# Attention and top-2 expert kernel on one core: order of the shared and routed iterations, scatter pacing and offset loads

## The reference

```
q, k, v = x Wq' + bq, x Wk' + bk, x Wv' + bv     # 8 query heads, 2 key/value heads of 16
attn    = softmax over the last 32 positions, with a sink term in the denominator
x       = layernorm(x + attn(q, k, v) Wo' + bo)
shared  = (silu(x sw1) * (x sw2)) sw3            # 128 -> 256 -> 128
probs   = softmax(x rw + rb); keep the best 2 of 8 experts, weights scaled to sum 1
routed  = sum over the 2 experts of weight * (silu(x ew1) * (x ew2)) ew3
x       = layernorm(x + shared + routed)
```

## Time and profile before

| what | us |
|---|---|
| three timed runs | 234.68, 229.27, 235.91 |
| their median | 234.68 |
| the profiled execution, its own time | 228.97 |
| its span, first to last instruction | 227.2 |
| PE busy | 171.9 (76% of the span) |
| POOL busy | 98.6 (43%) |
| mean granted TensorE clock | 0.932 of full speed |

### The profile page before, as it was taken

The page is one execution under the profiler, slowest core; times in us unless marked ns, Lnnn a source line. Parts: engine busy times, 40 slices in busy tenths (PEclk is TensorE's granted clock), DMA queues, the critical chain, the costliest instruction groups (busy, mean ns, idle before and its releaser), DMA issues.

```text
span 227.2 us, 3459 instructions
## 1 busy us (share of the span) xinstructions
PE 171.9 (76%) x974; PEld 119.0 (52%) x974; DVE 111.8 (49%) x360; ACT 107.8 (47%) x229; POOL 98.6 (43%) x110
## 2 busy tenths in 40 slices
PE   7499598698686657699678999999999899960000
PEld 2096577677574534456345656566666465650000
DVE  7875498589659929658123112121221221894070
ACT  2578968867945521312023555565556455650000
POOL 8440001006722766635700156465565544688330
PEclk9969999999999996999799999999999999996555
DMA  5995000000110111426530022333322036003310
GB/s 114 356 437 228 3 1 1 3 0 12 54 32 0 40 54 35 117 62 139 134 82 0 3 69 61 110 94 84 77 61 70 12 103 210 15 21 115 109 57 23
DMA packets 19458, 18.17 MB, mean 80 GB/s; under 512 B 3027, under 2 KB 17754, under 8 KB 19312
## 3 DMA queue, kind: packets, MB, share of 16 engines
q1 hardware_dynamic: 16432, 13.28, 20.2%
q0 software_dynamic: 2496, 4.24, 5.9%
q10 hardware_dynamic: 512, 0.45, 0.6%
HBM read 11.47 MB, written 7.39 MB: 83 GB/s over the span
## 4 chain that ended last, share of the span: by engine, by line
PE 47%; DVE 15%; issue 12%; POOL 7%; ACT 6%; DMA 5%; another core or an unknown queue 4%; ACTq 1%; POOLq 0%; DVEq 0%; SPq 0%
PE gu L574 18%; PE att L472 5%; POOL z_rows L1202 5%; PE q_bank L612 4%; PE att L586 3%; PE att L612 3%; PE att L566 3%; DMA bias<-biases 3%; PE q_bank L597 3%; PE att L552 2%; PE att L488 2%; ACT qT L706 2%; DVE mx L884 2%; DVE x L933 2%
## 5 line engine op out<-in xcount | busy, mean ns | idle before, releaser
L1202 POOL DMA_INDIRECT z_rows<-y,xin x46 | 45.6, 992 | 48.2 <-ACT y L790 36.6
L574 PE MATMUL gu<-w,xt 128*128 x92 | 45.7, 617 | 4.1 <-DVE h L1037 1.2
L1040 DVE TENSOR_TENSOR h<-sil,gu 128x512 f32<-128x512 f32 (+1 forms) x24 | 15.9, 663 | 61.8 <-ACT sil L776 57.1
L1194 POOL DMA_INDIRECT x_list<-x,pos x32 | 31.4, 981 | 16.5 <-issue 8.5
L776 ACT ACTIVATE sil<-gu 128x512 f32<-128x512 f32 (+1 forms) x24 | 13.9, 579 | 29.1 <-PE gu L574 26.8
L574 PEld LDWEIGHTS gu<-w,xt 128*128 128x128 f32 x92 | 15.5, 189 | 19.9 <-issue 19.9
L472 PE MATMUL att<-kM,qT 96*128 96x128 f32 x128 | 17.6, 297 | 8.2 <-ACT kM L719 3.6
L472 PEld LDWEIGHTS att<-kM,qT 96*128 96x128 f32 x128 | 16.4, 209 | 9.7 <-issue 9.7
L488 PE MATMUL att<-vbd,probT 128*128 128x128 f32 x128 | 17.1, 282 | 4.2 <-ACT probT L751 2.9
L1166 POOL TENSOR_TENSOR vareps<-mv,eps 128x4 f32<-128x4 f32 x4 | 0.8, 200 | 44.6 <-DVE mv L926 44.6
L488 PEld LDWEIGHTS att<-vbd,probT 128*128 128x128 f32 x128 | 15.3, 191 | 6.0 <-issue 3.6
(11 more groups left out here) (116 smaller groups left out, 289.0 us busy)
## 6 DMA issues: line engine op xcount, KB each, us to landing
w<-weights SPq DMA_DIRECT2D x1, 3456.0 KB, 16.6
xin<-x_list SPq DMA_DIRECT2D x46, 65.0 KB
z<-z_rows SPq DMA_DIRECT2D x3, 512.0 KB
x_list<-blank SPq DMA_DIRECT2D x18, 65.0 KB, 2.4
out<-result SPq DMA_DIRECT2D x3, 256.0 KB, 2.3
z_rows<-y,xin POOLq DMA_INDIRECT x46
xT<-x_cols SPq DMA_DIRECT2D x2, 256.0 KB, 5.7
xr<-x_rows SPq DMA_DIRECT2D x2, 256.0 KB, 7.0
```

What stands on the lines that cost most here:

```text
L574: mm = pe.matmul(gu_half[q], xt[:, pair % 2, q * P:(q + 1) * P], w[:, bass.ds(at[first_tile(pair) + q], CT)], start=True, stop=True)
L1040: dve.tensor_tensor(blocks(h[:, i % RING, 0:n * HIDDEN], HIDDEN), blocks(sil[:, i % 2, 0:n * HIDDEN], HIDDEN), blocks(gu[:, 0:n * CT], CT) ...
L1194: pool.indirect_dma_start(x_list[PART_OF[n]][:, :], bass.IndirectOffsetOnAxis(ap=pos[:, n, k, j:j + 1], axis=0), x2[:, n * ROWT + j, k * R ...
L1202: pool.indirect_dma_start(z_rows[g][:, :], bass.IndirectOffsetOnAxis(ap=xin[:, r, q, R_ID:R_ID + 1].bitcast(U32), axis=0), y[:, r, q, :], ...
```

## The change

1. The two shared iterations of chunk 3 go from iterations 6 and 7 to 30 and 31, behind the last pair. Pairs are now iterations 6 to 29; their number, and the 32 iterations, are the same. The first of the two moved iterations uses the banks post and att[3], the second gu; their sums go to x_bank (att[0]) instead of q_bank. PE does down_routed of the last pair ahead of the last up_shared, ACT scales the last two pairs in iteration 31, and add_shared(3) stands behind DVE's loop.
2. In scatter(n) POOL waits, ahead of the fifth of the 8 DMAs, until the first four of this chunk have landed.
3. PE loads the weight offsets for each pair (2 values, 24 loads), one iteration ahead, instead of 31 and 15 values at once.
4. rank(2) on PE goes ahead of the first up_shared. On DVE turn(3) goes ahead of read_ends(0), and make_table(0) goes from ahead of iteration 0 into iteration 1, behind hidden(1). The rest of chunk 3 (scale1, transpose, route, logits, rank, gates, places, table 1) goes one iteration later.
5. The combines of pieces 0 to 2 go to iterations 26, 27 and 28, scale2 to 28, 29 and 30; on POOL rstd2_of stands behind pairs 17, 18 and 19.

```diff
-SHARED_ITERS = 2 * CHUNKS
-R_AT = [SHARED_ITERS, SHARED_ITERS + PAIRS[0]]
-ITERS = R_AT[1] + PAIRS[1]
+FIRST_SHARED = 2 * (CHUNKS - 1)
+R_AT = [FIRST_SHARED, FIRST_SHARED + PAIRS[0]]
+R_END = R_AT[1] + PAIRS[1]
+ITERS = R_END + 2
...
-        gu_shared = [gu_half, [att[2][:, :], att[3][:, :]]]
+        turns = [gu_half, [att[2][:, :], att[3][:, :]]]
+        ends_banks = [[post[:, :], att[3][:, :]], gu_half]
...
+        SUMS_AT = R_AT[1] + 4
...
-            def fetch_weights(g):
-                pe.wait_ge(table_done, g + 1)
+            def fetch_weights(pair):
+                g, t = part_of(pair), first_tile(pair)
+                if t == 0:
+                    pe.wait_ge(table_done, g + 1)
                 _, values = nc.values_load_multi_w_load_instructions(
-                    table[g][0:1, T_W:T_W + TILES[g]], engines=PE_ONLY, min_val=0, max_val=SHARED * WRAW,
+                    table[g][0:1, T_W + t:T_W + t + width(pair)], engines=PE_ONLY, min_val=0, max_val=SHARED * WRAW,
...
             def up_shared(i, n, t):
                 pe.wait_ge(x2T_sb, n + 1)
                 after(pe, h_done, i - 1)
+                if i == R_END:
+                    pe.wait_ge(pos_done, CHUNKS)
+                    pe.wait_ge(step_done, 13)
...
+            rank(CHUNKS - 2)
             up_shared(0, 0, 0)
-            rank(CHUNKS - 2)
...
             for i in range(ITERS + 2):
-                if i == R_AT[0] - 1:
-                    at = fetch_weights(0)
-                if i == R_AT[1] - 1:
-                    next_at = fetch_weights(1)
-                if i + 1 < ITERS and pair_of(i + 1) is not None:
+                if pair_of(i + 1) is not None:
+                    at[i + 1] = fetch_weights(pair_of(i + 1))
                     turn_rows(pair_of(i + 1))
+                if i == ITERS - 1:
+                    down_routed(pair_of(i - 2), at[i - 2])
...
-                if i == 2:
+                if i == 3:
                     transpose_x2(last)
-                if i == 3:
+                if i == 4:
                     route(last)
-                if i == 4:
+                if i == 5:
                     rank(last)
...
-            read_ends(0)
             turn(last)
-            make_table(0)
+            read_ends(0)
             for i in range(ITERS):
                 hidden(i)
                 if i == 0:
                     norm1(last)
                 if i == 1:
+                    make_table(0)
+                if i == 2:
                     scale1(last)
-                if i == 3:
+                if i == 4:
                     logits(last)
-                if i == 4:
+                if i == 5:
                     gates(last)
                     places(last)
                     read_ends(1)
                     make_table(1)
...
-                if R_AT[1] + 5 <= i < R_AT[1] + 8:
-                    combine(i - R_AT[1] - 5)
-                if i == R_AT[1] + 7:
-                    scale2(0)
-            scale2(1)
-            scale2(2)
+                if SUMS_AT <= i < SUMS_AT + 3:
+                    combine(i - SUMS_AT)
+                if SUMS_AT + 2 <= i < SUMS_AT + 5:
+                    scale2(i - SUMS_AT - 2)
+            add_shared(last)
...
                 for j in range(first, last):
                     for k in range(2):
+                        if (j, k) == (2, 0):
+                            pool.wait_ge(scattered[PART_OF[n]], 16 * (2 * ROWT * PARTS[PART_OF[n]].index(n) + 4))
...
             for pair in range(PAIRS[0] + PAIRS[1]):
                 scatter_results(pair)
-                if PAIRS[0] + 3 <= pair < PAIRS[0] + 6:
-                    rstd2_of(pair - PAIRS[0] - 3)
+                piece = pair + FIRST_SHARED + 3 - SUMS_AT
+                if 0 <= piece < 3:
+                    rstd2_of(piece)
```

More of the change, by code:

```diff
@@ L114, in shared_of @@
 def shared_of(i):
-    return (i // 2, i % 2) if 0 <= i < SHARED_ITERS else None
+    if 0 <= i < FIRST_SHARED:
+        return i // 2, i % 2
+    return (CHUNKS - 1, i - R_END) if R_END <= i < ITERS else None
 def pair_of(i):
-    return i - SHARED_ITERS if SHARED_ITERS <= i < ITERS else None
+    return i - FIRST_SHARED if FIRST_SHARED <= i < R_END else None
 def part_of(pair):
@@ L565, in up_shared @@
                 for part in range(2):
-                    mm = pe.matmul(gu_shared[i % 2][part], w[:, at + part * HIDDEN:at + part * HIDDEN + P], x2T[:, tokens(n)],
+                    mm = pe.matmul(gu_shared(i)[part], w[:, at + part * HIDDEN:at + part * HIDDEN + P], x2T[:, tokens(n)],
                                    start=True, stop=True)
@@ L574, in up_routed @@
                     mm = pe.matmul(gu_half[q], xt[:, pair % 2, q * P:(q + 1) * P],
-                                   w[:, bass.ds(at[first_tile(pair) + q], CT)], start=True, stop=True)
+                                   w[:, bass.ds(at[q], CT)], start=True, stop=True)
                 mm.then_inc(up_mm, 1)
@@ L593, in down_shared @@
                         pe.wait_ge(q_sb, queries_done(CHUNKS - 1))
-                    after(pe, base_done, n)
+                    if n == CHUNKS - 1:
+                        pe.wait_ge(xt_sb, PAIRS[0] + PAIRS[1])
+                    else:
+                        after(pe, base_done, n)
                 at = SHARED * WRAW + DOWN + t * D
                 for j in range(ROWT):
-                    mm = pe.matmul(q_bank[:, j * D:(j + 1) * D], h[:, i % RING, j * P:(j + 1) * P], w[:, at:at + D],
+                    mm = pe.matmul(shared_sums(n)[:, j * D:(j + 1) * D], h[:, i % RING, j * P:(j + 1) * P], w[:, at:at + D],
                                    start=t == 0 and j == 0, stop=t == 1 and j == ROWT - 1)
@@ L690, in _ @@
                     down_shared(i - 2, *shared_of(i - 2))
-                elif pair_of(i - 2) is not None:
-                    down_routed(pair_of(i - 2), at if i - 2 < R_AT[1] else next_at)
+                elif pair_of(i - 2) is not None and i < ITERS - 1:
+                    down_routed(pair_of(i - 2), at[i - 2])
         @block.scalar
@@ L763, in rows_turned @@
                 act.wait_ge(xt_mm, pair + 1)
-                after(act, up_mm, SHARED_ITERS + pair - 1 if pair >= 2 else 0)
+                after(act, up_mm, FIRST_SHARED + pair - 1 if pair >= 2 else 0)
                 n = width(pair) * P
@@ L772, in silu @@
                 if shared_of(i) is not None:
-                    act.activation(sil[:, i % 2, :], gu_shared[i % 2][0], ACT.Silu).then_inc(silu_done, 1)
+                    act.activation(sil[:, i % 2, :], gu_shared(i)[0], ACT.Silu).then_inc(silu_done, 1)
                 else:
@@ L780, in hidden_turned @@
                 act.wait_ge(ht_mm, pair + 1)
-                after(act, down_mm, SHARED_ITERS + pair - RING + 1 if pair >= RING else 0)
+                after(act, down_mm, FIRST_SHARED + pair - RING + 1 if pair >= RING else 0)
                 n = width(pair) * HIDDEN
@@ L835, in _ @@
             last = CHUNKS - 1
-            for i in range(ITERS + 3):
+            for i in range(ITERS):
                 if pair_of(i + 1) is not None:
@@ L840, in _ @@
                     rows_out(i - 3, pair_of(i - 3))
-                if i < ITERS:
-                    silu(i)
-                if i == 2:
+                if i == ITERS - 1:
+                    rows_out(i - 2, pair_of(i - 2))
+                silu(i)
+                if i == 3:
                     x2T_out(last)
@@ L1131, in _ @@
             places(last - 1)
+            turn(last)
             read_ends(0)
-            turn(last)
-            make_table(0)
             for i in range(ITERS):
```

20 lines of the change are left out of this document (13 added, 7 removed).

## The result

The changed kernel takes 219.17 us in the median of four runs (217.12 to 223.27), the kernel before 231.98 in four (228.25 to 235.91). The ratio is 0.951, with a 95% interval of 0.939 to 0.962: 5% faster, some 12 us. The forecast was 219, 0.92 on faster.

What follows compares the result with a forecast made beforehand. PE alone bounds pair 0 to 20 (70.6 us), with holes before it and POOL's scatters in the tail. Pair 0 starting 13.0 us earlier takes 228.97 to 216.0; 2.9 for the median gives 219, range 212 to 228.

Steps and rivals of the forecast that it cites:

- The sum: Whole kernel: 13.0 us off 228.97, from pair 0 starting at 104.0 instead of 116.96, gives 216.0.
- The 2.9 added for the median: Whole kernel: half of the 5.7 us by which the median lay above the profiled execution, making 219.
- The rows' chain: Ahead of pair 0: table 0, POOL's scatters, first load of rows at 96.6 instead of 100.11, rows there at 99.2.
- the pause: POOL's scatters: waiting after four frees PE's held signals, removing gaps of 3.5 and 3.3 us; 1 lost to 5.1 gained.
- Deferred iterations: Chunk 3's two shared iterations, moved behind the last pair: 5.5 us gained before pair 0, hidden in the tail.
- Offsets by pairs: PE's 24 small loads during the pairs: 0.34 us for two values, all hidden; bounds 0 to 12.7 us.
- the hole at 108.5: PE's idle spell at the load of 31 offsets, with the slow clock after it: 4.5 us gained.
- The check's terms: Ahead of pair 0: 5.5 us shared iterations, 4.5 hole with slow clock, 3.0 earlier rows, as a check on 13.0.
- The rival of held signals that stay: Before chunk 3's ranks: pause doesn't remove the gaps, only 5 to 7 us gained, 226 us; chance 0.25.
- Between pairs 0 and 1: Start of the pairs: 0.5 us added because DVE has places(3) and table 1 between two iterations' products.

Runs made afterwards that it cites:

- e6: The changed kernel, same code, run and profiled again: 217.93 us in the profiled execution, median 217.78, ratio 0.950.
- e12: The changed kernel with up_shared(5), rank(3), down_shared(3) ahead of turn_rows(0), silu(5) ahead of rows_turned(0), make_table(0) ahead of iteration 0, pause kept: 0.966, median 216.94 us.
- e7: The changed kernel with chunk 3's shared iterations put back to iterations 6 and 7: median 224.59 us, profiled execution 222.21.
- e3: The kernel before with only the offsets loaded by pairs: ratio 0.988 (0.979 to 0.996).
- e4: The changed kernel with the 31 and 15 offsets loaded at once again: ratio 0.965 (0.952 to 0.977).
- e5: The kernel before, unchanged, run again for its trace: 233.38 us.
- e2: The changed kernel without the pause in the scatters: ratio 0.963 (0.952 to 0.975).
- e10: The changed kernel without the pause, run again in a later call: ratio 0.959 (0.952 to 0.966).
- e11: The changed kernel without the pause, with up_shared(5), rank(3), down_shared(3) ahead of turn_rows(0), silu(5) ahead of rows_turned(0), make_table(0) ahead of iteration 0: 0.946, median 211.73 us.
- e9: The kernel before with the pause alone, run again in a later call: median 227.22 us beside 229.59 for the kernel before.
- e1: The kernel before with only the pause after four scatters added: ratio 1.010 (1.003 to 1.017), some 2 us slower.

## Why the prediction was right, point by point

**The sum.** Forecast 216.0 for an execution like the profiled one; e6, which is one, took 217.93. Pair 0 begins at 105.21, forecast 104.0. From pair 0 to 20 there are 71.6 instead of 70.6, from there to the last scatter 23.3 instead of 23.7: 11.75 - 1.0 + 0.4 are the 11.0 us between 228.97 and 217.93, within 0.2. So the sum was 1.9 us too low. The 2.9 added for the median was too much: the median of 219.17 is 1.2 above e6. That 219 was met within 0.2 is luck, two errors that cancel.

**The rows' chain.** Table 0 was ready at 87.95 (forecast 88.5), last scatter of part 0 issued at 94.53 (93.8), first load of rows at 97.55 (96.6), rows there at 100.2 (99.2). That PE would then wait for rows, 3.0 us forecast, was 2.56. Right, with a shift of 0.7 to 1.0 from POOL. A part of it is the pause of chunk 2: I had booked nothing for it, and POOL waited 0.93 us (90.63 in e6), 3.28 in e12.

**Deferred iterations.** Forecast 5.5 us gained and hidden in the tail. e7 puts the move at 4.3 to 4.9 us, 5.4 in front less 1.2 between pairs 0 and 1, and PE's 5.6 us more work stands in a fourth stretch of unchanged length. The shared sums of chunk 3 are ready at 198.4 in e6, 6.7 us before z is there. Right.

**Offsets by pairs.** Taken as hidden: right (e3, pitch 3.57). The size of one load was off, 0.54 us at the median for 0.34; I had drawn a line through loads of 15 and 31. The Trainium skill's floor of about 600 ns ("DMA: Bandwidth & Descriptors", section "Latency and other measured facts") isn't a floor here: in e6 the two loads of a single value took 309 and 312 ns, and those of two values 532 or more. What I booked as a check, 4.5 us for the hole at 108.5, measured 2.7 with 1.9 of uncertainty alone (e3, on a chip without gaps), and in e4, within the change, the wait for rows covers the large load. The check's terms added up to 13.0 partly by luck: in the changed kernel they overlap.

**The step that was right on one kind of chip only is the pause.** I wrote that PE's signals are held while more than four scatters are issued in a row. Where the gaps exist, the two waits of the normalise bear that out: both are in the kernel before in two traces, neither is in the four traces of kernels with the pause, the first goes with no other edit ahead of it (e5 and e6), and a late signal stands where eight come in a row again. The rule itself is too simple even there. Two signals sent during the sixth scatter arrived at once (85.34 in e6, 115.36 in e5). One that was 1.7 us late was sent during the fourth of a row of result scatters (165.54, told at 167.23 in e6). Eight of the late ones are told within 0.2 us of the end of POOL's unbroken work, rstd1_of(3) included, but one in e5 came 0.69 us before it, and silu(0) in the first profile starts 1.4 us behind it (85.33). And e2, e3, e10 and e11 issue eight or more in a row and have no gap at all, so something that differs between chips or calls is needed too. What holds the signals stays open; since the ends of matmuls are modelled, the traces can't even tell a late signal from matmuls that really ended later. How much the pause alone brings on a chip with gaps wasn't measured, since e9 and e10, meant for it, ran on one without. On those chips it brings nothing that the runs show: 1.0% lost in e1, nothing that can be told in e9, 1.8 us from e2 to e4, 2.0% from e11 to e12. I had bounded that loss by 1 us, and it goes up to 4: POOL's batches for chunks 1 and 2 lie back to back, so the pauses go into the landing of part 0's last rows, and that of chunk 2, taken as free, waits 0.9 to 3.3 us.

**The rival of held signals that stay**, priced at 226, didn't come where it could have. On a chip without gaps the gain of the change seems to be less than there. The changed kernel itself wasn't run on one; e4, which differs in the loads alone, had 0.965.

**Between pairs 0 and 1** I took 0.5 us for DVE's table 1; it was 1.5 of idle PE, and it is the 0.9 that the third stretch is longer.

## What to carry to other kernels

Work that nothing waits for until the end goes where another engine is the bound: two iterations of TensorE's work behind the last pair cost nothing there and gave back 5.4 us in front of pair 0. An in-order engine that must wait for a transfer should first be given what doesn't need it; e11 does so and stands at 0.946 where the kernels without this edit and without the pause stood at 0.963 and 0.959, though e11 also moves table 1's wait out of the pairs, and the two effects weren't separated. A step taken as free because something else fills it (the pause behind rstd1_of(3)) needs the length of both: the fifth scatter came up to 5.6 us behind the fourth, not 2.4. And a long wait with no visible cause that is part of the price of a step should be looked for on a second chip before an edit is made against it.

## What the runs showed of the hardware that I had not expected

- TensorE's signals reach the other engines up to 3.95 us behind the recorded (modelled) end of the matmuls (e5, 64.74 to 68.69) in some calls, with the same code, beside a row of indirect DMAs from GpSimd; in others there is no such wait. The kernel before takes 7.6 us more at its best where they occur (228.6 against 221.0), 4.4 more than on another chip without them (224.2). The cause stays open.
- The same kernel may run its attention part with TensorE at 1.2 GHz for some 3 of the first 50 us (e6, mean granted clock 0.97) or for 17 of the first 52 (the first profile of the changed kernel), though the instructions are the same; the two executions took 217.93 and 223.27 us. The kernel before has the same two forms: 228.97 with the first profile (0.97), 233.38 in e5, with some 13 us at the low clock in its first 55.
- A register load on TensorE's queue takes some 310 ns for one value and 532 to 951 ns for two (e3, e6), and none of the 24 shows in the pitch of the pairs, 3.57 us in e3.
- POOL's wait for the landing of the same four scatters isn't the same for each chunk: in e12 the fifth follows the fourth after 2.6 us in chunks 0 and 1 and after 5.6 us in chunk 2.
